# Context stage of a gated cross-attention kernel: the row norms move one chunk later, and copies and loads are put in another order around them

## What is computed

```python
x = x + tanh(g_xattn[0]) * matmul(fake_quant(layernorm(x)), fake_quant(ctx))      # a
x = x + tanh(g_ffn[0])   * (quant_per_token(layernorm(x)) @ W.T + bias)           # b, W = W_int * block scales
x = x + tanh(g_xattn[1]) * (softmax(q @ k.T / sqrt(32)) @ v) @ Wo                 # q = layernorm(x) @ Wq
x = x + tanh(g_ffn[1])   * (layernorm(x) @ W4.T)                                  # k = ctx @ Wk, v = ctx @ Wv
```

## Time and profile before

| what | us |
|---|---|
| time, median of 3 runs | 863.67 |
| the three runs | 857.62, 863.67, 865.52 |
| the profiled execution, its own time | 859.74 |
| its span, first to last instruction | 857.9 |
| the context stage in it: first v product to first product of a | 9.5 to 125.7 |
| PE busy over the span | 826.9 (96%) |
| DVE, POOL, ACT busy over the span | 589.9, 535.6, 448.3 |

### The profile page before, as it was taken

One profiled execution on the slowest core, in us unless ns is written; L12 is line 12 of the kernel. 1 busy time (PEld: TensorE's weight loads), 2 busy tenths in 40 slices (PEclk: granted clock), 3 DMA queues, 4 the chain that ended last, 5 costly groups with the idle time before them and its releaser, 6 DMA issues.

```text
span 857.9 us, 14034 instructions
## 1 busy us (share of the span) xinstructions
PE 826.9 (96%) x4498; PEld 333.9 (39%) x4498; DVE 589.9 (69%) x850; ACT 448.3 (52%) x741; POOL 535.6 (62%) x235
## 2 busy tenths in 40 slices
PE   8799899899999999999999999999999989999998
PEld 7467644344444432222222222222222213444443
DVE  6886848988488557888888888888888500455622
ACT  4445445555322147777777777777777772111200
POOL 6455329966442417888889888888988886211200
PEclk9989999999999989999999999999999999999999
DMA  7999943336995213554464455456454334122341
GB/s 251 308 241 265 210 150 106 97 86 117 238 228 167 92 59 84 106 127 108 109 133 104 107 103 126 95 125 132 101 113 99 81 68 99 23 52 49 60 137 73
DMA packets 120822, 107.81 MB, mean 126 GB/s; under 512 B 85324, under 2 KB 105804, under 8 KB 116684
## 3 DMA queue, kind: packets, MB, share of 16 engines
q1 hardware_dynamic: 115120, 71.59, 32.1%
q0 software_dynamic: 4608, 33.56, 19.4%
q10 hardware_dynamic: 1052, 2.10, 0.8%
HBM read 41.55 MB, written 12.58 MB: 63 GB/s over the span
## 4 chain that ended last, share of the span: by engine, by line
PE 65%; POOL 10%; issue 7%; DMA 7%; POOLq 3%; DVE 3%; ACT 2%; DVEq 1%; ACTq 0%
PE sbank L1670 10%; PE sbank L1661 9%; PE mpair L1601 9%; POOL wraw L599 6%; DMA tail<-wraw 5%; POOLq L493 3%; PE sbank L1471 3%; PE sbank L1472 3%; PE sbank L1473 3%; PE sbank L1737 3%; PE sbank L1741 3%; PE sbank L1752 3%; PE sbank L1754 3%; PE sbank L1739 3%; POOL xT_lo L494 2%
## 5 line engine op out<-in xcount | busy, mean ns | idle before, releaser
L1333 DVE TENSOR_REDUCE mx<-mpair 128x1 f32<-128x1024 f32 x256 | 302.2, 1216 | 64.2 <-PE mpair L1601 63.2
L891 ACT ACTIVATE regC<-sbank 128x512 f32<-128x512 f32 x512 | 278.1, 594 | 107.6 <-PE sbank L1661 105.6
L1661 PE MATMUL sbank<-regD 98*128 98x512 f16 x512 | 179.5, 386 | 7.9 <-ACT regC L891 5.6
L599 POOL TENSOR_TENSOR wraw<-regC 128x2048 f32<-128x2048 f32 x32 | 148.9, 4652 | 28.6 <-DMA tail<-wraw 17.6
L1601 PE MATMUL mpair<-regD 96*128 96x512 f16 x512 | 157.3, 383 | 0.9 <-DVE mx L1333 0.3
L1670 PE MATMUL sbank<-regC,regD 128*32 128x512 f32 x1024 | 137.2, 608 | 1.0 <-ACT regC L891 1.0
L1661 PEld LDWEIGHTS sbank<-regD 98*128 98x128 f16 x512 | 48.7, 97 | 187.2 <-ACT regC L891 145.9
L599 POOL TENSOR_TENSOR regD<-regC 128x2048 f32<-128x2048 f32 x16 | 75.6, 4727 | 19.5 <-ACT regC L891 19.5
L599 POOL TENSOR_TENSOR tail<-regC 128x2048 f32<-128x2048 f32 x16 | 76.8, 4801 | 0.2 <-ACT regC L891 0.2
L1601 PEld LDWEIGHTS mpair<-regD 96*128 96x128 f16 x512 | 48.0, 98 | 55.1 <-DVE mx L1333 13.8
L492 POOL TENSOR_SCALAR xT_lo<-xT_lo,sc 128x1024 f32<-128x1024 f32 x16 | 30.1, 1878 | 43.7 <-DVE X L1001 35.4
(11 more groups left out here) (185 smaller groups left out, 1255.4 us busy)
## 6 DMA issues: line engine op xcount, KB each, us to landing
regD<-wraw POOLq DMA_DIRECT2D x16, 1024.0 KB, 7.0
tail<-wraw POOLq DMA_DIRECT2D x16, 1024.0 KB, 6.9
xT_lo<-in_ctx SPq DMA_DIRECT2D x16, 512.0 KB, 4.7
wraw<-in_L_ffn_W_int SPq DMA_DIRECT2D x8, 512.0 KB, 4.7
X<-in_x SPq DMA_DIRECT2D x4, 1024.0 KB, 7.2
wraw<-in_L_xattn_Wq SPq DMA_DIRECT2D x8, 512.0 KB, 3.7
wraw<-in_L_xattn_Wo SPq DMA_DIRECT2D x8, 512.0 KB, 4.3
regD<-q_hi_scratch SPq DMA_DIRECT2D x32, 128.0 KB, 2.4
```

Of the source, the lines that this page charges most:

```text
L599: nc.gpsimd.tensor_tensor(p_sum[pr if pr < 3 else 1][:, :, :], probs[:, (2 * pr) % 4, :, :], probs[:, (2 * pr) % 4 + 1, :, :], ALU.add).th ...
L891: nc.scalar.activation(probs[:, kt % 4, h, :], bank[4 + h % 2], ACT.Exp, scale=SCALE).then_inc(s["exp_ok"], 1)
L1333: v.tensor_reduce(mx[m][:, bass.ds(n, 1)] if par is not None else mx[m][:, n:n + 1], slot[:, :, :], AX.XY, ALU.max).then_inc(s["mx_red"], 1)
L1661: pe.matmul(bank[4 + h % 2], kst[par][0:98, kt * P:(kt + 1) * P], qst[par][0:98, h * 512:(h + 1) * 512], start=True, stop=True).then_inc(s ...
```

## The change

PE's program is untouched. All edits reorder the other queues in the context stage. The same instructions run; a semaphore `x_in3` is added, so that each load of x has its own.

- Rows of x: the pair for chunk c was loaded and normed in chunk c; now pair c-1 is loaded at the end of SP's turn c-1 and normed in chunk c. Chunk 0 has none, the last chunk has two pairs.
- ACT and DVE: the weight copies `wd_high(2c+1)`, `wd_low(2c+1)` and the key copy of half 0 now stand ahead of the row norms; on DVE the statistics of the second tile stand behind them. `turned_high` and `turned_low` of tile 8 move from chunk 1 into chunk 0, ahead of `consts()`. `ctx_high(u+3)` and `ctx_low(u+3)` stay behind the root and DVE's `ln1_affine`. In the last chunk `c2_out` moves ahead of the norms of the last pair, and `ln1_round(7)`, `ln1_out(7)` behind the last key copy.
- SP: `after_wd(2c+1)` moves ahead of the last two context loads, the load of x and both `xt1`; `scale4` is loaded at the stage's end.

```diff
@@ sync, chunk loop
-                if c == 0:
-                    sp.dma_start(X[:, 2:4, :], x_v[:, 2:4, :]).then_inc(x_in[1], 16)
                 ctx_turn(u + 2)
                 after_wd(2 * c)
                 if u + TB < U:
                     load_ctx(u + TB + 1)
                 store_v(c)
                 ctx_turn(u + 3)
+                after_wd(2 * c + 1)
                 if u + TB < U:
                     load_ctx(u + TB + 2)
-                xt1(2 * c)
-                if c == 1:
-                    sp.dma_start(X[:, 4:6, :], x_v[:, 4:6, :]).then_inc(x_in[1], 16)
-                    sp.dma_start(scale4[:, :, :], scales4.rearrange("(w p) b -> p w b", p=P)).then_inc(s["sc4_in"], 16)
-                if u + TB < U:
                     load_ctx(u + TB + 3)
-                after_wd(2 * c + 1)
-                xt1(2 * c + 1)
+                load_x(c)
+                if c > 0:
+                    xt1(2 * c - 2)
+                    xt1(2 * c - 1)
...
-            sp.dma_start(X[:, 6:8, :], x_v[:, 6:8, :]).then_inc(s["x_in2"], 16)
+            load_x(NCH - 1)
             store_k(NCH - 2)
             after_wd(6)
             store_v(NCH - 1)
+            xt1(T - 4)
+            xt1(T - 3)
+            after_wd(7)
             xt1(T - 2)
-            after_wd(7)
             xt1(T - 1)
+            sp.dma_start(scale4[:, :, :], scales4.rearrange("(w p) b -> p w b", p=P)).then_inc(s["sc4_in"], 16)
             store_k(NCH - 1)
@@ scalar, first_chunk and chunk
                 ctx_high(TB + 2)
-                ln1_root(0)
                 k_out(0, 1, True)
-                ln1_affine(0)
                 wd_high(1)
                 ctx_high(TB + 3)
-                ln1_out(0)
-                ln1_affine(1)
-                ln1_out(1)
+                turned_high(2 * TB, 6)
...
-                ln1_root(c)
-                ln1_affine(2 * c)
-                v_out(c, 3, first)
+                v_out(c, 3, False)
+                k_out(c, 0, False)
+                wd_high(2 * c + 1)
+                ln1_root(c - 1)
                 ctx_high(u + 3)
-                ln1_out(2 * c)
-                k_out(c, 0, first)
-                ln1_affine(2 * c + 1)
-                wd_high(2 * c + 1)
-                ln1_out(2 * c + 1)
-                k_out(c, 1, first)
+                ln1_affine(2 * c - 2)
+                ln1_out(2 * c - 2)
+                ln1_affine(2 * c - 1)
+                ln1_out(2 * c - 1)
+                k_out(c, 1, False)
@@ scalar, last chunk
+            ln1_root(c - 1)
+            ln1_affine(T - 4)
             v_out(c, 3, False)
+            ln1_out(T - 4)
+            ln1_affine(T - 3)
+            k_out(c, 0, False)
+            ln1_out(T - 3)
             ln1_root(c)
-            k_out(c, 0, False)
+            for n in range(2 * B):
+                c2_out(n)
             ln1_affine(T - 2)
+            wd_high(T - 1)
             ln1_out(T - 2)
             ln1_affine(T - 1)
-            for n in range(2 * B):
-                c2_out(n)
-            wd_high(T - 1)
+            k_out(c, 1, False)
             ln1_out(T - 1)
-            k_out(c, 1, False)
@@ vector, first_chunk and chunk
-                dve.wait_ge(x_in[0], 16)
-                ln1_stats(0)
-                ln1_affine(0)
                 k_low(0, 1)
                 wd_low(1)
                 ctx_low(TB + 3)
+                turned_low(2 * TB, 6)
                 ctx_round(TB + 2)
-                ln1_round(0)
                 wd_scale(2)
-                ln1_round(1)
                 ctx_round(TB + 3)
                 consts()
...
-                dve.wait_ge(x_in[1], 16 * c)
-                ln1_stats(c)
-                ln1_affine(c)
                 ctx_low(u + 2)
                 ctx_round(u + 1)
-                ln1_round(2 * c)
+                dve.wait_ge(x_in[c - 1], 16)
+                stats(2 * c - 2, 2 * c - 2)
+                k_low(c, 0)
+                wd_low(2 * c + 1)
+                stats(2 * c - 1, 2 * c - 1).then_inc(s["ln1_stat"], 1)
+                d()
+                ln1_affine(c - 1)
                 ctx_low(u + 3)
                 ctx_round(u + 2)
-                k_low(c, 0)
-                ln1_round(2 * c + 1)
-                wd_low(2 * c + 1)
+                ln1_round(2 * c - 2)
                 wd_scale(2 * c + 2)
+                ln1_round(2 * c - 1)
                 ctx_round(u + 3)
                 k_low(c, 1)
@@ vector, last chunk
             wd_low(T - 2)
+            ln1_stats(c - 1)
+            ln1_affine(c - 1)
             wd_scale(T - 1)
-            dve.wait_ge(s["x_in2"], 16)
+            ln1_round(T - 4)
             ln1_stats(c)
+            ln1_round(T - 3)
+            k_low(c, 0)
             ln1_affine(c)
-            k_low(c, 0)
             ln1_round(T - 2)
-            ln1_round(T - 1)
             wd_low(T - 1)
             k_low(c, 1)
+            ln1_round(T - 1)
```

More of the change, by code:

```diff
@@ L181, in build @@
         names = """pool_gate act_gate small_in wsc_in sc4_in bias_in wkv0 wkv1 wkv2 wkv3
-            cin0 cin1 cin2 cin3 win0 win1 x_in0 x_in1 x_in2 praw_in
+            cin0 cin1 cin2 cin3 win0 win1 x_in0 x_in1 x_in2 x_in3 praw_in
             ident_ok ones_ok small_mm sc_ok zp_ok gates_ok consts_ok bias_ok
@@ L204, in build @@
         win = [s["win0"], s["win1"]]
-        x_in = [s["x_in0"], s["x_in1"]]
+        x_in = [s[f"x_in{i}"] for i in range(4)]
         q_st = [s["q_st0"], s["q_st1"]]
@@ L302, in _ @@
             load_ctx(5)
-            sp.dma_start(X[:, 0:2, :], x_v[:, 0:2, :]).then_inc(x_in[0], 16)
             load_ctx(6)
@@ L313, in after_wd, with load_x @@
                     load_w(wq_v, w - (KD - 2), w % 2)
+            def load_x(p):
+                pair = slice(2 * p, 2 * p + 2)
+                sp.dma_start(X[:, pair, :], x_v[:, pair, :]).then_inc(x_in[p], 16)
             for c in range(NCH - 1):
@@ L747, in first_chunk, with chunk @@
                 ctx_high(TB + 2)
-                ln1_root(0)
                 k_out(0, 1, True)
-                ln1_affine(0)
                 wd_high(1)
                 ctx_high(TB + 3)
-                ln1_out(0)
-                ln1_affine(1)
-                ln1_out(1)
-            def chunk(c, first=False):
+                turned_high(2 * TB, 6)
+            def chunk(c):
                 u = TB * (c + 1)
-                turned_high(u, 6)
+                if c > 1:
+                    turned_high(u, 6)
                 ctx_high(u + 1)
-                v_out(c, 0, first)
-                v_out(c, 1, first)
-                v_out(c, 2, first)
+                v_out(c, 0, False)
+                v_out(c, 1, False)
+                v_out(c, 2, False)
                 wd_high(2 * c)
                 ctx_high(u + 2)
-                ln1_root(c)
-                ln1_affine(2 * c)
-                v_out(c, 3, first)
+                v_out(c, 3, False)
+                k_out(c, 0, False)
+                wd_high(2 * c + 1)
+                ln1_root(c - 1)
                 ctx_high(u + 3)
-                ln1_out(2 * c)
-                k_out(c, 0, first)
-                ln1_affine(2 * c + 1)
-                wd_high(2 * c + 1)
-                ln1_out(2 * c + 1)
-                k_out(c, 1, first)
+                ln1_affine(2 * c - 2)
[3 more added lines that the diff above has]
+                k_out(c, 1, False)
             first_chunk()
@@ L1117, in ln1_stats @@
             def ln1_stats(c):
+                dve.wait_ge(x_in[c], 16)
                 stats(2 * c, 2 * c)
@@ L1145, in chunk @@
                 u = TB * (c + 1)
-                turned_low(u, 6)
+                if c > 1:
+                    turned_low(u, 6)
                 ctx_low(u + 1)
```

## The result

| | before | after |
|---|---|---|
| time, median (lowest to highest of 14 runs each) | 861.99 (857.62 to 865.52) | 857.44 (855.78 to 859.92) |
| the profiled execution, its own time / its span | 859.74 / 857.9 | 856.11 / 854.3 |
| product a starts | 125.72 | 120.40 |

The ratio is 0.9955 [0.9942, 0.9968]: 4.5 us faster, half of the 8.9 forecast, and within 1% of before. The profiled executions differ by 3.6 us.

The account below looks back on a forecast made before the run. The context stage was taken as PE-bound apart from holes queueing on DVE. A gain of 13.7 - 1.3 (new wait) - 3.5 (DMA) = 8.9 us from 861.7 gave 852.8, said as 853, range 845 to 861.

Parts of the forecast that it names:

- Holes 1 to 3: PE's context-stage waits on DVE: 38.2 to 42.9 us, 1.8 us for turned tile 8, 98.0 to 101.4; all close.
- the table load: ACT's square-root table load, 1.28 us, falls at 54.9 where ACT waits for statistics until 57.3; costs nothing.
- the later bias load: Last chunk: bias load lands about 13 us after product a starts, `bias_scale` ran 16.8 after; costs nothing.
- the new wait: Chunk 1: `turned_low(12)` ends at about 69.1 where PE wants `wd_turn(4)` at 67.8; 1.3 us lost.
- The ceiling of 13.7: PE's work after 38.2 us sums to 73.8, so product a could start at 112.0, not 125.7: 13.7 at most.
- The rate: DMA per chunk: 5.2 MB of copies and eight 0.26 MB transposes take 27.2 us against PE's 23.5.
- the signs that it named itself: Right if product a starts between 113 and 119; wrong if later than 120 or PE waits on tiles 11 or 15.
- the DMA term: A DMA backlog makes the key store late and PE pays in the stage's last third; 0 to 6.7, taken 3.5 us.
- I count no clock drop for it: No half clock after PE's chunk 1 wait at `wd_turn(4)`, since the clock held at 1.00 around another 3.4 us wait; 0 us.
- so POOL starts adding earlier: Last chunk: `c2_out` ends 4 us ahead of product a, so POOL's additions start earlier; no cost counted.
- The rival with POOL's collisions: Stage ab: earlier POOL additions collide with DVE, four times 1.9 us; gain 1.4, time 860; chance 0.13.
- DMA keeps up: Rival for the context stage: transfers take 22.6 us per chunk, under PE's 23.5; gain 12.4, time 849.3; chance 0.30.

Follow-up runs that it names:

- three_b: Same program as `three`, run again in a later set: changed kernel with the edits of `storek`, `xearly` and `c2later`; 851.82 us, ratio 0.9902.
- xplus: Changed kernel with 1 MB more to move in chunk 1: the third pair of x loaded twice; 859.81 us, ratio 0.9986.
- xearly: Changed kernel with the load of the first pair of x (1 MB) issued at about 20 us instead of 44; 855.99 us, ratio 0.9932.
- storek: Changed kernel with SP's key store of chunk c-1 moved ahead of the transposes of tile u+1; 855.29 us, ratio 0.9946.
- turn12: Changed kernel with the copies of turned context tile 12 directly behind those of tile 11, ahead of the norms' other steps; 859.22 us, ratio 0.9986.
- c2later: Changed kernel with ACT's four column-sum copies behind `ln1_affine(6)` instead of ahead, so POOL starts adding later; 855.28 us, ratio 0.9941.
- three: Changed kernel with the edits of `storek`, `xearly` and `c2later` together; 850.48 us, ratio 0.9868.
- kearly: Changed kernel with the edits of `xearly` and `c2later`, key half 1's copies ahead of the affine steps, key store at SP's turn end; 856.13 us, ratio 0.9943.
- all4: Changed kernel with the edits of `storek`, `xearly`, `c2later` and `turn12` together; 855.11 us, ratio 0.9922.
- wdonly: Kernel before with only the load of weight tile 2c+3 moved ahead of the last context loads, x and `xt1`; 856.87 us, ratio 0.9949.

## Why the prediction was wrong, and what of it held

**Right.** Holes 1 to 3 closed, the clock stayed at 1.00 from 38 to 67, the table load (at 59.03 now) and the later bias load (131.88, `bias_scale` at 141.84) cost nothing, and the new wait came at the named place, `wd_turn(4)` for `turned_low(12)`. The ceiling of 13.7 was sound: less the losses below it gives the measured start of product a. No wait on tiles 11 or 15 came. The rate too: 7.3 MB in 27.2 us per chunk is 268 GB/s, and 275 was measured at a share of 1.13 from 38.1 to 67.7.

By the signs that it named itself it was wrong: product a starts at 120.40, outside of 113 to 119 and past 120.

**Wrong, the place of the DMA term and the size of the wait (4.8 us together; measured 5.8).** The sentence that failed is "It makes the key store late, `k_out(2,0)` waits for it ... and PE pays in the last third of the stage". The backlog was already there in chunk 1. The load of x stood in front of the transposes of tile 9, these in front of `store_k(0)`, and `k_out(1,0)`, which the hand schedule had right behind `k_proj(1,0)` at 53.0, came at 57.44. `three_b`, with the key copy right behind PE, still waits 2.50 us. So of the 5.76 some 2.5 us belong to the order on ACT and DVE (predicted 1.3), and the other 3.3 to the late key store, a difference of two executions: close to the 3.5 of the DMA term in size, 30 us earlier in place. `xplus` and `xearly` show that the megabytes ahead count, `storek` that SP's order counts too, and `turn12` that the last third pays when PE has not lost the time before.

**Wrong, "I count no clock drop for it".** This is the term that was furthest off: put at 0, measured 2.5 us. The 5.76 us wait was followed by half clock until 78.6. The 3.4 us of hole 3, on which I leaned, was a single case, and shorter. Product a: 13.7 - 5.8 - 2.5 = 5.4 earlier; measured 5.3.

**Wrong, the end of the stage ("so POOL starts adding earlier", at no cost).** The rival with POOL's collisions had the right two engines but put them in stage ab and made them 1.9 us each on wide instructions. They came before, on instructions of two columns, in the chain that frees the bank of a(1): 2.24 us of wait and 1.7 of half clock. Of the 5.3 us at product a, 1.2 were left when PE began a(2) (131.41 for 132.62). Later 2.6 came back, at a(6): the wait is 2.82 us for 3.73 and the clock did not fall after it (3.61 for 5.30 us). PE's next product, one of b, starts 3.8 us earlier (165.47 for 169.28), and the spans end 3.6 apart. Those 2.6 us are why the loss at the end of the stage does not count in full, and they may be why `c2later` gains 2.4 where a(1) alone had lost 3.9.

| term | predicted | measured |
|---|---|---|
| holes and half clock removed | 13.7 | about 13.7 |
| wait for `turned_low(12)` | -1.3 | -5.8 (order about 2.5, key store about 3.3) |
| DMA, elsewhere | -3.5 | 0 |
| half clock behind the wait | 0 | -2.5 |
| end of the stage | 0 | -3.9, then +2.6 in stage ab |
| gain in the profiled executions | 8.9 | 3.6 (4.5 by the medians) |

The measured terms add up to 4.1; the 0.5 to the profiled gain is less than what single executions differ by. Of the 4.8 us between forecast and measured terms, 2.5 are the half clock, 1.3 the end of the stage and 1.0 the wait.

**DMA keeps up**, the rival with 0.30, fell with `xplus` and `xearly`. The Trainium skill (DMA: Bandwidth & Descriptors, 🔬 Latency and other measured facts, and Where 436 GB/s comes from) had led to an estimate of 22.6 us per chunk, or 323 GB/s. This kernel moved 8.1 MB in the 29.6 us from 38.1 to 67.7 (275 GB/s) at a DMA share of 1.13, so over this stretch the mixed traffic ran slower than the page's separate rates, and the measurement decides. The same rival named a share of 0.37 to 1.07; its own rows reach 1.44 from 98.0 to 101.4, so the queue was fuller than it said.

**Open.** `three` still waits 2.4 us behind the order on ACT and DVE, and no run here takes that away without a wait later on. The queue sets other waits too (`kearly`: 2.33 us for the last pair of x), and at what backlog it stops doing so isn't known. Nor is it shown why a wait is followed by half clock in one execution and not in another (below), or why `all4` is slower than `three` by more than the stage shows.

## What to carry to other kernels

When work is packed closer on a core, count what is ahead in the DMA queue at each store that frees a buffer, not only the megabytes of a whole stage: the first victim is the first buffer whose release stands behind a large load, and moving its issue forward helps only in part if the load is already in the queue (`storek`: issued 7.1 us earlier by the clock, some 2.4 us gained). Take a wait away only after looking for the next in-order queue that has the same lateness in it (`turn12`), and try the smallest part of a change alone first (`wdonly` was worth as much as all of it). An engine that begins earlier should be checked against the small dependent instructions of the engine that shares its memory: two instructions of two columns lost 4.2 us here, where the two wide ones behind them lost 0.7 and 0.8 each.

## What the runs showed of the hardware

- DVE instructions of two columns took 2.32 and 2.23 us beside POOL's additions, and 0.16 and 0.23 with POOL idle; one addition takes 2.4. The Trainium skill (Trainium Architecture — The Big Picture, What this means for kernel authors) says that DVE and POOL contend for a shared pair of ports by an exclusive lock. The trace agrees with that picture for these two: each took about as long as one addition. It doesn't hold for all that DVE does beside POOL. In `c2later` L1203's two of 512 columns took 1.40 us together beside the additions, against 0.74 for one in the earlier trace rows, and L1101, at 125.51 in the kernel after, took 0.69 as at 58.07 with POOL idle. Those two read a product of PE (`mpair`, `sbank`); what decides was not tried.
- A transpose held SP for 1.23 us at the least (at 109.05 in `three_b`) and for 4.2 to 6.1 behind the load of x and two context tiles. A 256 KB store landed after 3.0 us, or after 10.0 with 2.5 MB issued just ahead of it.
- After idle times of PE of 5.76 and 3.56 us the next turn ran at half clock (1.94), after 2.38 and 3.26 the clock held (1.06 and 1.09), after 2.50 and 3.38 it fell in the middle of the turn (1.17 in `three_b`, 1.44 in `storek`), and after 3.89 (`kearly`) the turn took 1.07 but the matmuls behind it 0.42 for 0.27. But a(1) ran at half clock after 2.24 us in the kernel after (5.31) and at full clock after 2.25 in `xearly` (3.63), and a(6) at half clock after 2.32 in `c2later` (5.30) and at full clock after 2.32 in `xearly` (3.61). The length of the wait alone doesn't decide.
